# The down product of a sparse feed-forward as float16 pairs, one unit later, with byte masks

## The reference

```
def _sparsify_2to4(h):
    g = h.reshape(B, S, I // 4, 4)
    _, idx = jax.lax.top_k(jnp.abs(g), 2)
    ...                                   # keep the two largest of each four
h = silu(x @ w_gate) * (x @ w_up)         # 256 -> 1024
ffn = _sparsify_2to4(h) @ w_down          # 1024 -> 256
...
h = _layernorm(x) * (1 + cb) + sb
x = x + gb * ffn(h)
```

## Time and profile before

| | us |
|---|---|
| median of 3 runs | 2004.88 (2004.57 to 2007.66) |
| the profiled execution | 2004.2 |
| its span | 2002.5 |
| PE busy | 1949.4 (97%) |
| DVE busy | 1800.9 (90%) |
| ACT busy | 1742.7 (87%) |
| POOL busy | 1376.1 (69%) |

### The profile page before, as it was taken

One profiled execution on the slowest core, in us unless ns is written; L12 is line 12 of the kernel. 1 busy time (PEld: TensorE's weight loads), 2 busy tenths in 40 slices (PEclk: granted clock), 3 DMA queues, 4 the chain that ended last, 5 costly groups with the idle time before them and its releaser, 6 DMA issues.

```text
span 2002.5 us, 63709 instructions
## 1 busy us (share of the span) xinstructions
PE 1949.4 (97%) x24518; PEld 1660.5 (83%) x24518; DVE 1800.9 (90%) x2907; ACT 1742.7 (87%) x3591; POOL 1376.1 (69%) x957
## 2 busy tenths in 40 slices
PE   7799999999999999999999999999999999997899
PEld 6578888888888888888888888888888888886787
DVE  7789999999999999999999999999999999986997
ACT  7599999999999999999999999999999999896332
POOL 5467777777777777777777777777777777764452
PEclk9799999999999999999999999999999999999999
DMA  3000000000000000000000000000000000002100
GB/s 118 12 24 3 3 24 3 24 2 24 3 24 3 24 2 6 21 3 24 3 24 3 24 3 24 3 24 2 3 24 3 24 2 3 24 18 87 36 17 22
DMA packets 18013, 36.02 MB, mean 18 GB/s; under 512 B 5804, under 2 KB 14508, under 8 KB 15412
## 3 DMA queue, kind: packets, MB, share of 16 engines
q1 hardware_dynamic: 17716, 31.95, 4.8%
HBM read 29.30 MB, written 2.64 MB: 16 GB/s over the span
## 4 chain that ended last, share of the span: by engine, by line
PE 93%; DVE 3%; issue 1%; ACT 1%; POOL 1%; DMA 0%; SPq 0%; POOLq 0%; DVEq 0%; ACTq 0%
PE bank L658 83%; PE bank L661 10%; DVE cc L1864 0%; DVE tt L1739 0%; DMA osq<-in_x 0%; DVE y_acc L2029 0%; DVE b_le L1729 0%; DVE yl L1932 0%; DVE cols L1823 0%; DVE ae L1903 0%; DVE maskT L1764 0%; ACT inv L1435 0%; POOL a L556 0%; POOL invT L563 0%; ACT sq L1557 0%
## 5 line engine op out<-in xcount | busy, mean ns | idle before, releaser
L1864 DVE SCALAR_TENSOR_TENSOR cc<-bank,wc,cc 128x510 f32<-128x510 f32 (+2 forms) x768 | 559.2, 740 | 11.2 <-ACT cc L1350 1.5
L658 PE MATMUL bank<-h,w 128*128 128x512 f16 (+1 forms) x1920 | 422.1, 360 | 1.1 <-DVE zg L1977 1.1
L658 PEld LDWEIGHTS bank<-h,w 128*128 128x128 f16 x1920 | 174.4, 98 | 136.0 <-issue 5.0
L1435 ACT ACTIVATE inv<-bank 128x512 f16<-128x512 f32 x384 | 244.6, 637 | 18.7 <-PE bank L658 18.7
L491 POOL TENSOR_TENSOR rn<-n2m,mhalf 128x4 f32<-128x4 f32 x64 | 64.5, 1007 | 274.7 <-DVE n2m L1877 274.7
L1440 ACT ACTIVATE invT<-bank 128x512 f16<-128x512 f32 x384 | 246.5, 642 | 2.1 <-PE bank L658 2.0
L1932 DVE TENSOR_TENSOR yl<-bank,mask 128x512 f16<-128x512 f32 x320 | 219.0, 684 | 5.7 <-PE bank L658 5.6
L658 PE MATMUL bank<-inv,a 128*128 128x64 f16 (+1 forms) x3584 | 218.4, 197 | 2.9 <-ACT inv L1435 2.9
L1350 ACT ACTIVATE cc<-bank,wc 128x512 f32<-128x512 f32 x256 | 177.7, 695 | 32.1 <-PE bank L658 32.1
L658 PE MATMUL bank<-w,goT 128*128 128x256 f16 x1536 | 190.3, 274 | 4.4 <-DVE goT L1984 4.4
L658 PEld LDWEIGHTS bank<-inv,a 128*128 128x128 f16 x3584 | 181.2, 98 | 15.0 <-ACT inv L1435 3.8
(11 more groups left out here) (232 smaller groups left out, 5505.6 us busy)
## 6 DMA issues: line engine op xcount, KB each, us to landing
w_raw<-in_wh SPq DMA_DIRECT2D x15, 1032.0 KB, 4.8
out<-sol SPq DMA_DIRECT2D x16, 128.0 KB, 1.7
v<-in_x SPq DMA_DIRECT2D x3, 512.0 KB, 3.8
moving<-rank_store SPq DMA_DIRECT2D x64, 8.0 KB
standing<-rank_store SPq DMA_DIRECT2D x64, 8.0 KB
w_raw<-in_wgate SPq DMA_DIRECT2D x1, 1024.0 KB, 4.9
...
```

What stands on the lines that cost most here:

```text
L658: return mm(o_, l_, r_, start=start, stop=stop, skip_group_check=True)
L1435: A(lefts(inv[:, ring(s)], l), halves(bL[0], l), ACT.Copy).then_inc(sig("x_ready"), 1)
L1864: V.scalar_tensor_tensor(dst, src, wc[:, par(s), i, 3 - j:4 - j], dst, ALU.mult, ALU.add).then_inc(sig(f"conv{i}"), 1)
```

## The change

- The down product takes float16 pairs: the selected values and the down weights (times 64) are each a high and a low half, and three products (high high, high low, low high) of four planes make 12 matmuls for a part where there were four float32 ones. It waits for the low half (`al`) and runs on tile u-3, one turn later; `gate_down` and `add_residual` go to tile u-4.
- ACT gets `selected_high(u)` (a copy of 128 x 1024 to float16) at the end of each turn; POOL gets `selected_low(u-1)` (128 x 1024, difference to float16) between `hidden_low` and `hidden_rstd`, held until `compare(u)` (`f_adj`) and `hidden_normed(u+4)` (`xn`) are done, and `add_input(u+5)` stands ahead of `hidden_low(u+3)`. The low half of the last unit is DVE's (`selected_low_last`).
- The down weights are split in the last call of `last_bodies`: two copies on ACT, two instructions of 128 x 1024 on DVE.
- `compare` writes bytes; `count` takes them two at a time as 16-bit words (so 256, 128, 128 and 512 elements instead of 512, 256, 256 and 1024), with 257 for one in each byte.
- The drain is re-ordered: on DVE `gated(0)`, `gated(1)` go ahead of `level_rows(1)`, `gated(2)`, `gated(3)` behind `second_rest`, the four `gate_weights_low` further back, and `count(0)`, `hidden_product(1)` behind the `output_low`s; PE does `gate(2)` in the last call instead of in the loop; POOL does `low_half` later. The first eight normed tiles get room of their own (four in `standing`).

```diff
-        f_s = [o[:].rearrange("p t v d -> p (t v d)"), flat(osq[:]), flat(zth[:]), flat(zg[:])]
-        f_adj, f_part, f_keep = (yl[:, i].rearrange("p u s -> p (u s)").rearrange("p (i n) -> p i n", i=PLANES)
-                                 for i in (2, 3, 4))
-        f_two = flat(yl[:, 5])[:, 0:512].rearrange("p (i n) -> p i n", i=2)
+        f_s = [o[:].rearrange("p t v d -> p (t v d)"), flat(osq[:])]
+        f_sp = [(flat(a1[:, 0]), flat(a_lo[:, 0])), (flat(a1[:, 1]), flat(a_lo[:, 1])),
...
+        f_adj, f_keep = (flat(yl[:, i])[:, 0:512].bitcast(U8).rearrange("p (i n) -> p i n", i=PLANES) for i in (2, 4))
+        f_two = flat(yl[:, 5])[:, 0:256].bitcast(U8).rearrange("p (i n) -> p i n", i=2)
+        f_adj2, f_part2, f_keep2 = (flat(yl[:, i])[:, 0:512].bitcast(U16).rearrange("p (i n) -> p i n", i=PLANES)
+                                    for i in (2, 3, 4))
+        f_two2 = flat(yl[:, 5])[:, 0:256].bitcast(U16).rearrange("p (i n) -> p i n", i=2)
...
+            def selected_low(u):
+                pool.wait_ge(sig("ah"), STEPS + u + 1)
+                gp.tensor_tensor(f_sp[u % 4][1], f_s[u % 2], f_sp[u % 4][0], ALU.subtract).then_inc(sig("al"), 1)
@@ PoolE, loop over the units
...
-                if u >= 3:
-                    add_residual(u - 3)
+                if u >= 4:
+                    add_residual(u - 4)
+                if u + 5 < NT:
+                    add_input(u + 5)
                 if 0 < u < NT - 3:
                     hidden_low(u + 3)
+                if u:
+                    pool.wait_ge(sig("f_adj"), u * 3 + 3)
+                    if u + 4 < NT:
+                        pool.wait_ge(sig("xn"), NT + u + 5)
+                    selected_low(u - 1)
                 if u + 5 < NT:
-                    add_input(u + 5)
                     hidden_rstd(u + 5)
-            for j in range(UNITS - 3, UNITS):
+            for j in range(UNITS - 4, UNITS):
                 add_residual(j)
@@ TensorE
...
                 u = j // 2 * 2 + hh
-                need(pe, "f_s", u + 1)
+                pe.wait_ge(sig("al"), STEPS + u + 1)
                 if first:
-                    pe.wait_ge(sig("wd_dma"), 16)
+                    pe.wait_ge(sig("f_w_lo"), 10)
                     pe.wait_ge(sig("ya"), STEPS * 2)
                     need(pe, "yo_mul", j - 1 if j > NT - 4 else j)
-                s_ = f_s[u % 4].rearrange("p (i n) -> p i n", i=PLANES)
+                s_ = [half_.rearrange("p (i n) -> p i n", i=PLANES) for half_ in f_sp[u % 4]]
+                o_ = bk[:, (j % 2) * C:(j % 2) * C + C]
                 for p_ in range(PLANES):
-                    ins = m(bk[:, (j % 2) * C:(j % 2) * C + C], s_[:, p_, j % 2 * P:j % 2 * P + P], wd_sb[:, 2 * p_ + hh, :],
-                            start=(first and p_ == 0), stop=(last and p_ == PLANES - 1))
+                    for n_, (a, b) in enumerate(((0, 0), (0, 1), (1, 0))):
+                        ins = m(o_, s_[a][:, p_, j % 2 * P:j % 2 * P + P], wd_parts[b][:, 2 * p_ + hh, :],
+                                start=(first and p_ == 0 and n_ == 0), stop=(last and p_ == PLANES - 1 and n_ == 2))
                 if last:
                     ins.then_inc(sig("down_ps"), 1)
...
                 turn_output(1, s3)
+                if not s2:
+                    gate(2)
                 bank_output(0, s0)
...
             for u in range(UNITS):
+                if 1 < u and u + 1 < UNITS:
+                    gate(u + 1)
                 if 0 < u and u + 1 < UNITS:
-                    gate(u + 1)
                     up(u + 1)
                 if 0 < u < NT - 3:
                     turn_hidden(u + 3)
-                if u >= 2:
-                    down(u - 2)
+                if u >= 3:
+                    down(u - 3)
+            down(NT - 3)
             for hh in range(2):
                 for j in (NT - 2, NT - 1):
                     down_part(j, hh, hh == 0, hh == 1)
@@ ScalarE
...
+            def down_weights_high(q):
+                act.wait_ge(sig("wd_dma"), 16)
+                act.wait_ge(sig("h_ps"), STEPS * 2)
+                act.wait_ge(sig("tm_ps"), STEPS * 2)
+                qs_ = slice(q * 1024, q * 1024 + 1024)
+                A(wd_flat[0][:, qs_], flat(ae[:, q]), ACT.Copy, scale=W_SCALE).then_inc(sig("w_hi"), 1)
+            def selected_high(u):
+                act.wait_ge(sig("f_s"), u + 1)
+                if u >= 2:
+                    need(act, "down_ps", (u // 2 - 1) * 2)
+                A(f_sp[u % 4][0], f_s[u % 2], ACT.Copy).then_inc(sig("ah"), 1)
...
                 if not s2:
                     magnitude(0)
+                    down_weights_high(0)
                     gate_silu(1)
+                    down_weights_high(1)
...
                     magnitude(u + 1)
+                selected_high(u)
@@ VectorE
...
+            def down_weights_low(q):
+                dve.wait_ge(sig("w_hi"), NK * 8 + 8 + q + 1)
+                qs_ = slice(q * 1024, q * 1024 + 1024)
+                V.scalar_tensor_tensor(wd_flat[1][:, qs_], flat(ae[:, q]), W_SCALE, wd_flat[0][:, qs_], ALU.mult,
+                                       ALU.subtract).then_inc(sig("f_w_lo"), 1)
...
                 dve.wait_ge(sig("f_adj"), u * 3 + 3)
-                V.scalar_tensor_tensor(f_part[:, 0:2], f_adj[:, 1:3], -1.0, f_two, ALU.add,
+                V.scalar_tensor_tensor(f_part2[:, 0:2], f_adj2[:, 1:3], ONE_EACH, f_two2, ALU.add,
                                        ALU.add).then_inc(sig("f_part"), 1)
-                V.tensor_tensor(f_part[:, 2], f_adj[:, 3], f_two[:, 0], ALU.subtract).then_inc(sig("f_part"), 1)
-                V.tensor_tensor(f_part[:, 3], f_adj[:, 0], f_two[:, 1], ALU.subtract).then_inc(sig("f_part"), 1)
+                V.scalar_tensor_tensor(f_part2[:, 2], f_adj2[:, 3], 2 * ONE_EACH, f_two2[:, 0], ALU.add,
+                                       ALU.subtract).then_inc(sig("f_part"), 1)
+                V.scalar_tensor_tensor(f_part2[:, 3], f_adj2[:, 0], 2 * ONE_EACH, f_two2[:, 1], ALU.add,
+                                       ALU.subtract).then_inc(sig("f_part"), 1)
                 dve.wait_ge(sig("f_part"), u * 3 + 3)
                 need(dve, "f_s", u)
-                V.tensor_tensor(f_keep, f_part, f_adj, ALU.subtract).then_inc(sig("f_keep"), 1)
+                V.tensor_tensor(f_keep2, f_part2, f_adj2, ALU.subtract).then_inc(sig("f_keep"), 1)
             def select(u):
...
-                need(dve, "down_ps", (u // 2 - 1) * 2)
+                if u >= 2:
+                    dve.wait_ge(sig("al"), STEPS + u - 1)
                 h4 = f_h[u % 2].rearrange("p (f n) -> p f n", f=PLANES)
-                s4 = f_s[u % 4].rearrange("p (f n) -> p f n", f=PLANES)
-                V.scalar_tensor_tensor(s4, f_keep, 0.0, h4, ALU.is_ge, ALU.mult).then_inc(sig("f_s"), 1)
+                s4 = f_s[u % 2].rearrange("p (f n) -> p f n", f=PLANES)
+                V.scalar_tensor_tensor(s4, f_keep, 2.0, h4, ALU.is_ge, ALU.mult).then_inc(sig("f_s"), 1)
+            def selected_low_last():
+                u = UNITS - 1
+                dve.wait_ge(sig("ah"), STEPS + u + 1)
+                dve.wait_ge(sig("al"), STEPS + u)
+                V.tensor_tensor(f_sp[u % 4][1], f_s[u % 2], f_sp[u % 4][0], ALU.subtract).then_inc(sig("al"), 1)
...
                 if s1:
+                    if not s0:
+                        gated(0)
+                        gated(1)
                     level_rows(1, s1)
-                    if not s0:
-                        for j in range(TL):
-                            gated(j)
-                        gate_weights_low(0)
...
                     if not s0:
-                        gate_weights_low(2)
-                        gate_weights_low(3)
+                        gated(2)
+                        gated(3)
...
+                if s1 and not s0:
+                    gate_weights_low(0)
+                    gate_weights_low(1)
...
                     compare(0)
                     hidden_stats(TL)
-                    count(0)
-                    hidden_product(1)
                 output_low(0, s3)
                 if s2:
                     up_weights_low(2)
                     up_weights_low(3)
                     hidden_product(0)
                 output_low(1, s3)
+                if not s2:
+                    down_weights_low(0)
+                    count(0)
+                    hidden_product(1)
+                    down_weights_low(1)
...
-                if u >= 3:
-                    gate_down(u - 3)
+                if u >= 4:
+                    gate_down(u - 4)
                 if u + 5 < NT:
                     gated(u + 5)
                 if u:
                     compare(u)
-                if u + 1 == UNITS:
-                    gate_down(u - 2)
                 if u + 4 < NT:
...
-            for j in range(UNITS - 2, UNITS):
+            selected_low_last()
+            for j in range(UNITS - 4, UNITS):
                 gate_down(j)
```

(5 more changed lines are left out.)

23 lines of the change are left out of this document (16 added, 7 removed).

## The result

The changed kernel takes 2008.55 us in the median of 22 runs, the one before 2004.65 (22 runs): a ratio of 1.0025, interval 1.0017 to 1.0032. One execution of each kernel ran far slower than the rest (2234.51 and 3291.23 us) and is left out of the ratio, which is one of means, so it is not quite the quotient of the medians, 1.0019. The change is slower by a little more than a measurement can tell from nothing; the forecast was 2009.5. The two profiled executions differ by less (spans of 2004.2 and 2002.5), since the attention part, whose code is the same, took 2.5 us less in the one of after: ACT's last copy of `ae` to `a_hi`, the last thing ahead of the drain that both have, starts at 1796.7 before and at 1794.1 after. The two rows are of all instructions of that line, before and after; the last number is the last start.

What follows compares the result with a forecast made beforehand. PE bounded the loop at 8.92 us a turn; the change makes DVE the bound at 9.3. Loop +5.6, drain -7.1 and end +6.2 give +4.7 on 2002.5; plus 1.7 and 0.7, 2009.5 us, range 2000.5 to 2015.

Steps and rivals of the forecast that it cites:

- DVE's own work: Loop: DVE's turn without holds falls from 7.40 to 6.86 us, with count's 512-word instruction at the double rate.
- Case D: Loop: 16-bit words run one a cycle in count, 4.1 us more, 2013.6 us; chance 9%.
- The holds: Loop, turns 4 to 10: four POOL instructions hold DVE for 0.53 + 0.5 + 0.4 + 1.0 = 2.43 us a turn.
- The loop: Turn 1 to the end of select(15): 130.6 us instead of 125.0, +5.6, with DVE as the bound.
- The drain: Ahead of the loop: two PE waits shrink, -7.1 us in sum, so turn 1 starts at 1863.2.
- the first place: Drain: PE's 4.16 us wait for level_rows goes and matmuls behind it run faster, 5.5 us earlier.
- the second: Drain: gate(2) moves into PE's 4.39 us wait for goT, 1.6 us gained; down_weights_low costs DVE nothing else.
- The end: After the last select: PE starts 2.8 us later, 48 matmuls take 7.1, then 3.5: 13.4 instead of 7.2, +6.2.
- The sum: Whole span: +5.6 - 7.1 + 6.2 = +4.7 us on 2002.5, so 2007.2.
- B: Holds of 1.9 instead of 2.43 us a turn, or the end at full clock: 2002 to 2008 us; chance 30%.
- E: The drain gives nothing, as displaced DVE instructions and weight splits fill the gap: 2012 to 2016.6 us; chance 7%.
- C: Loop: PE stays the bound, DVE's turn stays under 8.1 us, time 1997 us; chance 16%.

Runs made afterwards that it cites:

- drain_only: The kernel before with the changed drain alone (down product, masks and loop order stay): 1997.33 us, 0.9970.
- low_dve: The changed kernel with every low half on DVE, between hidden_product and count, and none on POOL: 2006.84 us, 1.0016.
- stats_first: The changed kernel with gate_down(12) and gate_down(13) earlier at the end and hidden_stats ahead of count: 2003.19 us, 0.9997.
- low_small: The changed kernel with POOL's selected_low cut to 64 of 1024 columns: 1992.55 us, 0.9949.
- bytes_only: The kernel before with the byte masks and the word counts alone: 2001.96 us, 0.9992.
- gated_together: The changed kernel with four gated ahead of the third level_rows instruction again and the four gate_weights_low where they were: 2014.95 us, 1.0051.
- masks_f16: The changed kernel with masks and counts in float16 as before, the bytes undone: 2015.41 us, 1.0062.

## Why the prediction was right, and where it was not

**DVE's own work, 6.86 us.** Right. `count`'s instruction of 512 words of uint16 is as fast as the double rate says (all instructions of the line in the changed kernel, ns min/median/max):

```profile
L2139 DVE TENSOR_TENSOR yl<-yl x16: 424/424/778, 1853.6 to 1989.1; 128x512 uint16<-128x512 uint16 x16
```

Case D is out. So the Trainium skill's condition ("VectorE: DVE Perf Modes", section "What auto-detection actually checks"), every tensor 16-bit with step ±1, agrees with these 424 ns. It does not carry over to `count`'s other instructions: a `scalar_tensor_tensor` of 16-bit words took 0.41 us for 256 elements and, in float16, 0.68 for 512 (drain_only), no faster an element than the float32 ones.

**The holds, 2.43.** Right in the sum (0.53 + 0.53 + 0.35 + 1.02), a little off in the parts: the two small ones are 0.88 where I had 0.9. The turn came out at 9.30. low_dve and stats_first moved the turn by what the hold says, and low_small by all that PE's 8.08 left room for. The exclusive lock that the Trainium skill speaks of ("SBUF — State Buffer", section "SBUF: two separate sides") agrees with `count`'s first instruction, which ended 0.28 us after `selected_low`; the cover by PSUM operands and by the statistics, 0.55 for 0.55, is what this case adds in numbers. `hidden_normed` was held although only one of its operands is a whole tile in SBUF (0.75 for 0.40), and the statistics, with one as well, were not (0.41); what makes the difference no run here shows. And I had PE wait for DVE's `hidden_product`: the 1.2 us are there, but the waits are for `gate_down` and `hidden_low`.

**The loop, +5.6.** Measured +5.3. Turns 1 to 3 were 8.8 to 8.9, 11 and 12 8.5 and 8.3, the last three 7.3.

**The drain, -7.1.** Measured -5.5 in the first place (26.7 to 21.2; 5.4 when undone by itself) and -1.7 in the second (19.7 to 18.0), for the 5.5 and 1.6 of the sum. Of the 5.5, up to 1.1 can be the length that the slowed stretch happened to have (bytes_only has 25.7 with the same order, gated_together 26.6). The size of the second was right and its step was not. I put it down to `gate(2)` in PE's wait, and called `down_weights_low` free. `gate(2)` alone gives nothing, the order of `count` and `hidden_product` alone gives nothing. The bound there is DVE's own work, once its 3.3 us of idle time are gone: drain_only has 16.3 (3.4 gained), the down weights' two instructions bring back about 2.3, and the shorter words take 0.5 off (masks_f16: 18.5), which leaves the 1.7 up to rounding. This account of the three terms fits the traces; no run takes the down weights' two instructions away by themselves. That a guess about PE hit a sum of three terms on DVE was luck.

**The end, +6.2.** Measured 13.4 against 7.2, as summed: PE starts 2.8 us after the last `select`, 7.1 us for 48 matmuls, 3.5 behind them. The reason for the slowed stretch was only partly right: I expected an idle time above 4 us, it was 2.5. low_small has 2.3 us idle at the same place and does the 48 in 5.4 us at a clock of 1.00. The changed kernel differs from it in a second thing, 3.4 us that PE waited for `gate_down(11)` 10 us earlier, with slowed matmuls behind it. Two traces speak against this one as the cause. masks_f16 has it more strongly (4.99 us idle, 48 matmuls in 7.9), and its last 48 are at full clock; low_dve has 2.98 us idle there with the matmuls behind it at full clock, and its last 48 take 7.1 us:

```profile
1995.38 0.37 PE L683 MATMUL bank<-inv,a 128*128 128x256 f16 x1 [4.99 <-DVE sol L2160]
2005.43 0.27 PE L683 MATMUL bank<-inv,standing 128*128 128x256 f16 x1 [1.87 <-DVE sol L2160]
```

```profile
1986.20 0.27 PE L679 MATMUL bank<-inv,a 128*128 128x256 f16 x1 [2.98 <-DVE sol L2162]
1994.81 0.27 PE L679 MATMUL bank<-inv,standing 128*128 128x256 f16 x1 [3.21 <-DVE sol L2162]
```

Ahead of the last 48, the idle times of 1.87 and 2.31 go with full clock and those of 2.46 and 3.21 with a slowed stretch, but low_dve's 2.98 went with full clock too. What decides is open, and with it 1.7 us of the 6.2.

**The sum.** The two traces differ by +4.2 from the copy on, where the sum had +4.7; the attention part ahead of it, 2.5 us shorter in the trace of after, is no part of the sum.

**The rivals.** B's smaller holds and D's slower words are refuted by the turn of 9.30, E by the drain. C is what low_small became once the low half was gone.
